# Adjacencies by spans of 40 destinations instead of blocks of 128, in a two-layer graph kernel on one Trainium2 core

## What is computed

```python
h = maximum(layernorm(x), 0)
# layer 0: edges 0-255 with W_hh (HH), 256-1535 with W_oo (OO), the rest with W_ho (HO)
e_f = relu(concat([h[src], h[dst]]) @ W + b)
logit = e_f @ W_a + b_a
ex = exp(logit - segment_max(logit, dst)[dst]);  alpha = ex / segment_sum(ex, dst)[dst]
z_f = segment_sum(alpha * h[src], dst)
x = x + relu(concat([h, z_f]) @ W_n + b_n)      # W_hn for nodes 0-127, W_on for the rest
# layer 1: c = w * rsqrt(w_out[src] * w_in[dst]), degrees clipped to >= 1
h = maximum(layernorm(x), 0)
agg = segment_sum((h * rsqrt(deg_out))[src] * c, dst) * rsqrt(deg_in)
x = x + relu(agg @ W_1 + b_1)
```

## Time and profile before

| | us |
|---|---|
| three timed runs, median (lowest, highest) | 662.76 (662.02, 662.83) |
| the profiled execution, of its own | 663.61 |
| its span in the trace | 660.8 |
| busy: PE, DVE, POOL, ACT | 579.9, 453.9, 224.3, 210.1 |

### The profile page before, as it was taken

One profiled execution on the slowest core, in us unless ns is written; L12 is line 12 of the kernel. 1 busy time (PEld: TensorE's weight loads), 2 busy tenths in 40 slices (PEclk: granted clock), 3 DMA queues, 4 the chain that ended last, 5 costly groups with the idle time before them and its releaser, 6 DMA issues.

```text
span 660.8 us, 8395 instructions
## 1 busy us (share of the span) xinstructions
PE 579.9 (88%) x2570; PEld 355.6 (54%) x2587; DVE 453.9 (69%) x770; ACT 210.1 (32%) x264; POOL 224.3 (34%) x210
## 2 busy tenths in 40 slices
PE   0999999999999798851999478999889899989997
...
GB/s 310 326 406 109 286 97 143 320 411 410 412 414 402 377 415 412 409 409 251 389 410 408 183 89 65 194 73 64 73 69 77 67 189 252 131 1 127 1 32 95
DMA packets 47256, 153.76 MB, mean 233 GB/s; under 512 B 6448, under 2 KB 7280, under 8 KB 47216
## 3 DMA queue, kind: packets, MB, share of 16 engines
...
## 4 chain that ended last, share of the span: by engine, by line
PE 46%; DVE 20%; DMA 16%; POOL 7%; issue 6%; ACT 1%; SPq 1%; DVEq 1%; ACTq 0%; POOLq 0%
PE banks L999 21%; DMA rows<-table,ids_i 13%; PE banks L1104 12%; POOL rows L404 7%; PE banks L1163 6%; DVE masked L714 6%; DVE rows L692 4%; PE banks L1180 3%; DVE rows L693 3%; DMA lift<-lift_row 1%; PE banks L1115 1%; PE banks L979 1%; DVE stage L726 1%; PE banks L1099 1%; DMA lift_row<-liftT 1%
## 5 line engine op out<-in xcount | busy, mean ns | idle before, releaser
L404 POOL DMA_INDIRECT rows<-table,ids_i x124 | 141.9, 1145 | 180.9 <-DMA table<-stage 84.2
L1019 PE MATMUL banks<-w_raw,fT_raw 128*128 128x512 f32 x384 | 168.3, 598 | 10.0 <-DMA w_raw<-in_L_gnn_W_hn_dram 3.9
L1019 PEld LDWEIGHTS banks<-w_raw,fT_raw 128*128 128x128 f32 x384 | 73.0, 192 | 104.7 <-issue 92.1
L692 DVE TENSOR_TENSOR rows<-rows 128x1024 f32<-128x1024 f32 x62 | 75.6, 1220 | 52.5 <-DMA rows<-table,ids_i 52.2
L1104 PE MATMUL banks<-pick_src,pick_dst 128*128 128x512 bf16 x403 | 102.7, 391 | 9.8 <-issue 4.3
L424 POOL DMA_INDIRECT pick_src<-eye_row,ids_i x64 | 65.1, 1017 | 90.7 <-PE banks L1107 66.1
L636 DVE TENSOR_TENSOR w_lo<-w_raw,w_hi 128x1024 fp32r<-128x1024 f32 x40 | 48.1, 1224 | 55.9 <-ACT w_hi L462 55.8
L999 PE MATMUL banks<-w_hi,fT_hi 128*128 128x512 f32 x200 | 77.9, 389 | 0.1
L999 PE MATMUL banks<-w_hi,fT_lo 128*128 128x512 f32 x200 | 77.8, 389 | 0.0
L999 PE MATMUL banks<-w_lo,fT_hi 128*128 128x512 f32 x200 | 77.8, 389 | 0.0
L693 DVE SCALAR_TENSOR_TENSOR rows<-rows,wa_rep 128x1024 f32<-128x1024 f32 x62 | 75.9, 1225 | 2.1
...
## 6 DMA issues: line engine op xcount, KB each, us to landing
...
```

The lines of the kernel that those rows point to most:

```text
L404: pool.indirect_dma_start(out=rows[:, slot, side, :], out_offset=None, in_=table[kind][side], in_offset=bass.IndirectOffsetOnAxis(ap=ids_i ...
L692: step(dve.tensor_tensor(rows[:, r, 0, :], rows[:, r, 0, :], rows[:, r, 1, :], ALU.add))
L1019: ins = pe.matmul(bank[j][:, :], fT_raw[:, k, m * P:(m + 1) * P], w_raw[:, c % SLOTS, n * H:(n + 1) * H], start=(k == 0), stop=(k == K - 1))
```

## The change

Each adjacency is made by 13 spans of 40 destinations. For a span the three parts lie side by side as 3 x 40 = 120 weight columns, so one matmul per edge tile adds all three; the tiles are taken in groups of eight from the first that reaches the span (`span_words` works out the first tile and how many further groups there are, two spans to a word). The result is 120 rows x 512 sources in bank 4 or 5. ACT copies it out (`keep_span`), and PE adds the three parts and transposes at once, with `span_sum` as weights and `fold_m`, three identities of 40 under one another, as moving operand (`fold_span`), into banks 0 to 3, which hold the transposed matrix of each pass in turn. The source one-hots of all 64 tiles are made once by ACT (`pick`), most of them beside the raw products, in space that is free by then; POOL's fetches and the table in HBM go. PE sums the degrees ahead of the first span (`degrees`). The in-sums and the sums of `ex` are made by PE out of the transposed matrices in bank 7, not by reductions on DVE. In the beginning ACT's queue loads the indices, the first norm goes block by block, and the index work is changed to match.

```diff
--- before.py
+++ after.py
+SPAN = 40
+GROUP = 8
...
-        pick_dst = [sb(f"pick_dst{r}", [P, 2, 3, N], BF16, over=at + r * pair_size)[0] for r in range(RING)]
-        pick_src = [sb(f"pick_src{r}", [P, 2, N], BF16, over=at + r * pair_size + 2 * 3 * N * 2)[0]
-                    for r in range(RING)]
...
+        pick_src, _ = sb("pick_src", [P, T, N], BF16, over=fT_at)
...
+        pick_dst = [sb(f"pick_dst{r}", [P, T, 3, SPAN], BF16, over=base)[0] for r, base in enumerate((tail, at))]
...
+        LAST_MAX, ME_PE, ME_DVE, PARTS, EXP = 4, 7, 9, 11, 7
+        FIRST_SRC, EARLY_SRC = 17, 3 * T // 8
+        SRC_PAIRS = [*range(T // 4, T // 2), *range(T // 8, T // 4), *range(T // 8)]
...
+        def span_code(eng, words, sp):
+
+            code = (words[sp // 2] >> (9 * (sp % 2))) & 511
+            return eng.snap(code & 63), eng.snap(code >> 6)
+
+        def group_at(eng, first, i):
+
+            return eng.snap(first + i * GROUP).with_bounds(max_val=T - GROUP)
...
-            for a, arr in enumerate((src, dst, edge_w)):
...
-            pool.wait_ge(hh_logits, TILE_HH)
-            for pair in range(T // 2):
-                fetch_one_hot(pair, 0)
-            for pair in range(T // 2):
-                fetch_one_hot(pair, T // 2)
...
+            for a, arr in enumerate((src, dst, edge_w)):
+                tgt = ids_row[:, a, :] if a < 2 else ids_rowf[:, a, :]
+                for i0, t0, n in RUNS:
+                    act.dma_start(tgt[i0:i0 + n], arr[t0 * P:(t0 + n) * P].rearrange("(t p) -> t p", p=P)).then_inc(ids_in, 16)
+
+            def relu(b):
                 act.wait_ge(h_pre, b + 1)
                 act.activation(xf[:, b, :], xf[:, b, :], ACT.Relu).then_inc(h_ready, 1)
+
+            relu(0)
+            relu(1)
+            hi(0)
+            relu(2)
+            relu(3)
             hi(1)
+            act.wait_ge(idsT_ready, 1)
+            act.activation(ids_f[:, :, :], bank[K - 1][:, 0:3 * T].rearrange("p (a t) -> p a t", a=3), ACT.Copy
+                           ).then_inc(ids_kept, 1)
+            act.activation(tile_row[:, :], bank[K - 1][0:1, 3 * T:5 * T], ACT.Copy).then_inc(ids_kept, 1)
...
+            def pick(n):
+
+                pair = SRC_PAIRS[n]
+                if n == 0:
+                    act.wait_ge(chunk_used, 2 * K)
+                else:
+                    act.wait_ge(src_made, n)
+                if pair == T // 8:
+                    act.wait_ge(fT_raw_done, K // 2)
+                if pair < T // 8:
+
+                    act.wait_ge(chunk_used, C_HH + K + pair + 1)
+                for r in range(2):
+                    i = tile_at(2 * pair + r)
+                    act.activation(pick_src[:, 2 * pair + r, :].bitcast(F16), node_no, ACT.Abs, bias=ids_f[:, 0, i:i + 1],
+                                   scale=-1.0).then_inc(own_act, 1)
+                act.wait_ge(own_act, 2 * n + 2)
+                both = pick_src[:, 2 * pair:2 * pair + 2, :]
+                act.activation(both, both.bitcast(F16), ACT.Relu, bias=ones_f[:, 0:1], scale=-1.0).then_inc(src_made, 1)
+
+            def keep_span(n):
+
+                act.wait_ge(span_full, n + 1)
+                if n >= 2:
+                    act.wait_ge(folded, n - 1)
+                act.activation(span_sum[n % 2][0:3 * SPAN, :], bank[4 + n % 2][0:3 * SPAN, :], ACT.Copy).then_inc(span_out, 1)
...
+                if FIRST_SRC <= c < FIRST_SRC + EARLY_SRC:
+                    pick(c - FIRST_SRC)
...
+            for pair in range(EARLY_SRC, T // 2):
+                pick(pair)
+            act.wait_ge(hh_logits, TILE_HH)
+            for n in range(SPANS):
+                keep_span(n)
+                if n == EXP:
                     act.wait_ge(arg_ready, 1)
                     act.activation(ex[:, :], me[:, :], ACT.Exp, scale=-1.0).then_inc(ex_ready, 1)
+                    act.wait_ge(deg_done, 1)
+                    act.activation(sums[:, :, :], bank[6][:, 0:4 * B].rearrange("p (b k) -> p b k", k=4), ACT.Copy).then_inc(sums_out, 1)
+            act.wait_ge(folded, SPANS)
+            for s in range(B):
+                act.activation(adjwT[:, s, :], bank[s][:, :], ACT.Copy).then_inc(adjwT_ready, 1)
+            for n in range(SPANS):
+                keep_span(SPANS + n)
+                if n % 2 == 1 and n < 2 * B:
+                    if n == 1:
+                        act.wait_ge(h_back, 16)
+                    b = n // 2
                     act.activation(hn_hi[:, b, :], hf[:, b, :], ACT.Copy).then_inc(hn_hi_done, 1)
+            act.wait_ge(folded, 2 * SPANS)
...
+            first_stats(0)
+            first_stats(1)
+            first_norm(0)
+            first_stats(2)
+            first_norm(1)
+            first_stats(3)
+            first_norm(2)
...
+                dve.tensor_tensor(reach[:, :, :], tiles(tile_row[:, T:2 * T]), each(lo_end), ALU.is_ge)
+                step(dve.tensor_tensor(other[:, :, :], each(hi_end), tiles(tile_row[:, 0:T]), ALU.is_ge))
+                step(dve.tensor_tensor(reach[:, :, :], reach[:, :, :], other[:, :, :], ALU.mult))
+
+                step(dve.scalar_tensor_tensor(other[:, :, :], tiles(q_row[:, :]), 1.0, reach[:, :, :], ALU.add, ALU.mult))
+                step(dve.tensor_reduce(last, other[:, :, :], AX.X, ALU.max))
+                step(dve.tensor_scalar(q_row[:, :], q_row[:, :], -1.0, float(T), ALU.mult, ALU.add))
+                step(dve.tensor_tensor(other[:, :, :], tiles(q_row[:, :]), reach[:, :, :], ALU.mult))
+                step(dve.tensor_reduce(first, other[:, :, :], AX.X, ALU.max))
...
+            span_words()
+            dve.tensor_copy(ones_r[:, :], ones_f[:, 0:1].broadcast_to([P, 4])).then_inc(ones_ready, 1)
+            split3(w_col, ids_f[:, 2, :])
...
+            def spread(n, col):
+
+                sp, slot = n % SPANS, n % 2
+                if n >= 2:
+                    dve.wait_ge(span_full, n - 1)
+                first, extra = span_code(dve, words, sp)
+                nodes = node_all[:, sp * SPAN:(sp + 1) * SPAN]
+                with dve.Fori(0, extra + 1) as i:
+                    q, at_pick = group_at(dve, first, i), group_at(dve, 0, i)
+                    dve.tensor_tensor(pick_dst[slot][:, bass.ds(at_pick, GROUP), 2, :],
+                                      nodes[:, None, :].broadcast_to([P, GROUP, SPAN]),
+                                      dst_q[:, bass.ds(q, GROUP), None].broadcast_to([P, GROUP, SPAN]), ALU.is_equal)
+                step(dve.memset(span_end[:, 2 * n:2 * n + 1], 0.0))
+                with dve.Fori(0, extra + 1) as i:
+                    q, at_pick = group_at(dve, first, i), group_at(dve, 0, i)
+                    picks = pick_dst[slot][:, bass.ds(at_pick, GROUP), :, :]
+                    dve.tensor_tensor(picks, pick_dst[slot][:, bass.ds(at_pick, GROUP), 2:3, :].broadcast_to([P, GROUP, 3, SPAN]),
+                                      col[:, bass.ds(q, GROUP), 1:4, None].broadcast_to([P, GROUP, 3, SPAN]), ALU.mult)
+                dve.memset(span_end[:, 2 * n + 1:2 * n + 2], 0.0).then_inc(span_ready, 1)
+
+            spread(0, w_col)
...
+            def exp_sums():
+
+                dve.wait_ge(den_done, 1)
+                dve.tensor_scalar(den[:, :], bank[7][:, 0:4 * B:4], TINY, None, ALU.max).then_inc(den_kept, 1)
+                dve.wait_ge(den_kept, 1)
                 dve.reciprocal(rden[:, :], den[:, :]).then_inc(rden_ready, 1)
...
+            def degrees():
+
+                regions = bank[6][:, 0:4 * B]
+                pe.matmul(regions, zeros[:, :], node_no[:, 0:4 * B], start=True, stop=True)
+                for q in range(T):
+                    for s in range(B):
+                        pe.matmul(bank[6][:, 4 * s:4 * s + 4], pick_src[:, q, s * P:(s + 1) * P], w_col[:, q, :],
+                                  start=False, stop=True, skip_group_check=True)
+                pe.matmul(regions, zeros[:, :], node_no[:, 0:4 * B], start=False, stop=True,
+                          skip_group_check=True).then_inc(deg_done, 1)
+
+            def add_span(n):
+
+                sp, slot, rows3 = n % SPANS, n % 2, slice(0, 3 * SPAN)
+                out_bank = bank[4 + n % 2]
+                first, extra = span_code(pe, words, sp)
+                if n >= 2:
+                    pe.wait_ge(span_out, n - 1)
+                pe.matmul(out_bank[rows3, :], zeros[:, rows3], node_no, start=True, stop=True)
+                pe.wait_ge(span_ready, n + 1)
+                with pe.Fori(0, extra + 1) as i:
+                    q, at_pick = group_at(pe, first, i), group_at(pe, 0, i)
+                    for j in range(GROUP):
+                        pe.matmul(out_bank[rows3, :], pick_dst[slot][:, bass.ds(at_pick + j, 1), :, :],
+                                  pick_src[:, bass.ds(q + j, 1), :], start=False, stop=True, skip_group_check=True)
+                pe.matmul(out_bank[rows3, 0:B], zeros[:, rows3], node_no[:, 0:B], start=False, stop=True,
```

(46 more changed lines are left out.)

351 lines of the change are left out of this document (128 added, 223 removed).

## The result

| | before | after | forecast |
|---|---|---|---|
| timed runs, median (lowest, highest) | 662.80 (662.02, 664.46), 4 runs | 640.05 (638.22, 643.41), 4 runs | 630.4 |
| the profiled execution, its span | 663.61, 660.8 | 641.69, 639.8 | 631.3, 628.5 |
| mean granted clock | 0.962 | 0.942 | |
| busy: PE, DVE, POOL, ACT | 579.9, 453.9, 224.3, 210.1 | 575.2, 419.2, 158.8, 211.0 | |
| stage, first to last | 377.2 to 520.8 | 378.3 to 491.8 | 375.6 to 484.7 |

After against before is 0.966 (95% interval 0.961 to 0.971). The adjacency stage is 113.5 us long where it was 143.6 and where 109.1 were forecast.

The account below looks back on a forecast made before the run. It took PE to bound the early products and the adjacency stage, DMA gathers the middle. Stage -34.5, denominators +3.8, beginning -1.6 gave -32.3 on 663.61: 631.3 profiled, 630.4 us timed; 8-in-10 range 612 to 652.

Parts of the forecast that it names:

- Span matmuls and folds: Adjacency stage on PE: 26 spans at 2.23 us, 58.0 us, and 26 folds at 1.0 us, 26 us.
- Rivals 3 and 4: Fold cost: 3, cheap, 0.5 us each, 613 us, chance 0.18; 4, dear, 1.6 us each, 650 us, chance 0.09.
- Degrees: 256 small matmuls ahead of the first span, at 0.026 us each: 6.7 us.
- node maxima: Piece of PE work inside the adjacency stage, taken as unchanged: 6.7 us.
- denominators: 32 fp32r matmuls of four columns on PE behind the features, at 0.12 us each: 3.8 us added.
- Stalls: PE waits in the stage: 1.5 us for DVE's maxima at span 4, 1.0 at the pass change, 2.5 together.
- the double buffer's cover: At span 4, some 4.5 us of buffering was set against DVE's 6 us of maxima, leaving 1.5 us of stall.
- The lower clock: Lower PE clock twice in the stage, after the idle time and after the node maxima: 4.6 us.
- The last copy: ACT's final copy out of PSUM at the end of the spans, counted in the stage at 0.8 us.
- The beginning: PE's stream starts at 19.2 us (-5.7), then waits for chunk 4 (+4.1): -1.6 us net, from -5.7 to +1.
- rival 2: DVE or address arithmetic sets the stage's pace: 4.0 us per span instead of 3.23, +19, 649 us; chance 0.10.
- Rival 1: PE clock stays at the lower level through the adjacency stage: +71 us, 701 us; chance 0.06.

Follow-up runs that it names:

- e8: Changed kernel with the last chunk's four blocks of edge maxima placed one each behind spans 2 to 5; 639.12 us, 0.966 of before.
- e12: Changed kernel with in-sums, denominator pieces and span words moved, most degrees started earlier, span 1's selection before the last-but-one chunk's maxima; 632.47 us, 0.955 of before.
- e1: Changed kernel with the last chunk's edge maxima split behind spans 3 to 6, the rest behind span 7 and later; 635.46 us, 0.956 of before.

## Why the forecast was 10 us too low

The profiled span was forecast at 628.5 and was 639.8. By the forecast's own steps:

- **Span matmuls and folds**, the two largest terms, were right. 2.23 + 1.0 = 3.23 us per span were taken; in the second pass twelve intervals took 37.94 us, 3.16 each. The pass of a fold is 0.115 us (0.12 taken). Rivals 3 and 4 fall with it. The bounds of the matmul were 0.213 and 0.227; it goes at 0.216, as those of before do (1.46 = 5 x 0.216 + 0.38 in the earlier trace rows). The Trainium skill's page "TensorE: Matmul & The Clock Gate", section "Weight-path perf modes", grants the fast load to exactly 128 weights that are not FP32, and the trace agrees: 139 ns busy for 120 columns against 99 for 128. What it would have made of the spans (0.227) did not come: under 512 moving columns the load of 139 ns, shorter than the 216 between matmuls, is hidden.
- **Degrees** 6.9 (6.7), **node maxima** 6.6 (6.7), **denominators** 3.5 (3.8): right.
- **Stalls** were put at 2.5 and are 8.2, 5.4 of them at span 5. The step that went wrong is the double buffer's cover: 4.5 us were set against 6 us of DVE's work. But span 5's own selection stands behind that work, so from the end of span 4's product (398.6) to span 5's (407.7) it is 9.1 us, against the 4.0 until TensorE came to span 5 (402.6).
- **The lower clock** was put at 4.6 us, twice in the stage. Behind the stall, behind the maxima and in span 0 the spans were 4.7 us longer than 1.89 each and two clearing matmuls 0.5, the in-sums 1.9 us over 3.8: 7.1. Outside the stage it was put at nothing and cost 3.2 behind the wait for chunk 4 (15.8 us at 0.80), 2.6 in the features and 1.7 behind the denominators. 14.6 in all, 10 more than forecast. With the stalls' 5.7 this is the miss, and by e8 the two are not independent: there the stall went and the clock fell. Part of it is this execution's own: behind the wait for chunk 4 the lower level cost 1.7 us and not 3.2 in six of the seven others with that beginning.
- **The last copy** (0.8) was hidden behind the last two folds.
- **The beginning**: the stream began at 18.8 (19.2), waited 2.9 for chunk 4 (4.1), and ended at 112.5, not at 110.7, for the clock behind that wait. Degrees began at 378.3 (375.6); they waited for ACT's last pairs, but e12 shows that this wait cost nothing.
- In the chain from the last edge block to span 5, the forecast added up TensorE; e12 shows that DVE's work sets the time there. So DVE sets the pace in the stage's first 30 us, as rival 2 had it for the whole, though not by its 4.0 us per span.
- **Rival 1**, the lower level through the stage, came true for a quarter of it (mean clock 0.88), 10 us of this in the degrees and span 0; the second pass was at 1.00.

The terms agree with the whole: start of the stage +2.7, inside it +4.4 (stalls 5.7, clock 2.5, spans and folds -1.8, last copy -0.8; 1.2 too much), behind it +4.2 (clock 4.3, denominators -0.3), together 11.3. By the medians of the timed runs, 640.05 against 630.4, it is 9.7.

What stays open: why e1 was faster by its times and not by its trace, what brings the clock down behind the same wait in one execution and not in another, and what sets how long a stretch at the lower level lasts.
